# A mixed feed-forward phase in smaller parts, with its partial sums kept on the chip

## The reference

```python
h = relu(x @ gate_w1.T + gate_b1)
g = (h @ gate_w2.T + gate_b2).mean(axis=1)          # 8 numbers for each batch
mW1 = W1 + einsum('be,efh->bfh', g, TW1)            # mixed weights, one set for each batch
mb1 = b1 + g @ Tb1
mW2 = W2 + einsum('be,ehf->bhf', g, TW2)
mb2 = b2 + g @ Tb2
u = gelu(einsum('bsh,bfh->bsf', x, mW1) + mb1)
out = einsum('bsf,bhf->bsh', u, mW2) + mb2
result = x1 + layernorm(out)                        # x1: the residual; the network's x is layernorm(x1)
```

## Time and profile before

| | us |
|---|---|
| median of 3 runs | 3212.77 (3205.09 to 3214.96) |
| the profiled execution, its time | 3212.9 |
| its span, first to last instruction | 3210.9 |
| PE busy in the span | 2959.3 (92%) |
| DVE busy | 2125.1 (66%) |
| ACT busy | 1229.8 (38%) |
| POOL busy | 788.1 (25%) |

### The profile page before, as it was taken

The page is one execution under the profiler, slowest core; times in us unless marked ns, Lnnn a source line. Parts: engine busy times, 40 slices in busy tenths (PEclk is TensorE's granted clock), DMA queues, the critical chain, the costliest instruction groups (busy, mean ns, idle before and its releaser), DMA issues. The chain is left out here.

```text
span 3210.9 us, 54877 instructions
## 1 busy us (share of the span) xinstructions
PE 2959.3 (92%) x20408; PEld 2436.0 (76%) x20408; DVE 2125.1 (66%) x3970; ACT 1229.8 (38%) x2354; POOL 788.1 (25%) x629
## 2 busy tenths in 40 slices
PE   7999999699999999689979898689998999999997
PEld 6888888588888888567757777578877887778886
DVE  4333332388878888587678788586868858595633
ACT  2222222266666766555422222222323223322232
POOL 0000000288878888633200000100011000100011
PEclk9999999799999999889979999899999999999999
DMA  5545554678777777599989999787977959597631
GB/s 190 177 163 194 179 170 163 161 185 194 193 180 193 195 193 190 148 330 360 350 328 404 403 397 374 253 328 259 366 257 280 371 212 341 215 352 260 223 131 66
DMA packets 441120, 796.72 MB, mean 248 GB/s; under 512 B 29105, under 2 KB 161201, under 8 KB 440889
## 3 DMA queue, kind: packets, MB, share of 16 engines
q1 hardware_dynamic: 440896, 793.73, 73.8%
HBM read 600.16 MB, written 192.94 MB: 247 GB/s over the span
## 5 line engine op out<-in xcount | busy, mean ns | idle before, releaser
L1435 DVE SCALAR_TENSOR_TENSOR e_part<-ring,e_g_cols,e_part 128x512 f32<-128x512 f32 x896 | 634.4, 771 | 37.8 <-DMA ring<-mix_rows 37.5
L1379 ACT ACTIVATE e_u<-e_hid,e_mb 128x512 f32<-128x512 f32 x256 | 176.5, 689 | 966.9 <-PE e_hid L1327 966.7
L666 DVE TENSOR_REDUCE b_neg_max<-b_ps_score 128x1 f32<-128x384 f32 (+1 forms) x1024 | 492.3, 527 | 72.9 <-PE b_ps_score L531 61.2
L1341 PE MATMUL e_acc<-e_w_hi,e_u_hi 128*128 128x512 f32 x1024 | 417.2, 407 | 105.9 <-DVE e_u_lo L1445 105.9
L1286 POOL TENSOR_TENSOR e_rows<-e_rows,e_prev 128x512 f32<-128x512 f32 x64 | 96.9, 1543 | 1496.4 <-DVE e_rows L1473 994.7
L637 ACT ACTIVATE b_probs<-b_ps_keys 128x384 f32<-128x384 f32 (+1 forms) x1024 | 427.0, 478 | 84.5 <-PE b_ps_keys L546 57.0
L1325 PE MATMUL e_hid<-e_y_hi,e_w_hi 128*128 128x512 f32 x1024 | 401.9, 392 | 10.9 <-DMA e_y_lo<-yl_scratch 8.6
L1342 PE MATMUL e_acc<-e_w_lo,e_u_hi 128*128 128x512 f32 x1024 | 410.4, 401 | 0.0
L1343 PE MATMUL e_acc<-e_w_hi,e_u_lo 128*128 128x512 f32 x1024 | 410.1, 401 | 0.0
L1326 PE MATMUL e_hid<-e_y_lo,e_w_hi 128*128 128x512 f32 x1024 | 400.8, 391 | 0.0
L1327 PE MATMUL e_hid<-e_y_hi,e_w_lo 128*128 128x512 f32 x1024 | 400.1, 391 | 0.0
(11 more groups left out here) (118 smaller groups left out, 4797.0 us busy)
## 6 DMA issues: line engine op xcount, KB each, us to landing
ring<-mix_rows SPq DMA_DIRECT2D x576, 512.0 KB, 7.9
qk_scratch<-a_qk SPq DMA_DIRECT2D x128, 512.0 KB, 2.8
b_k_st<-qk_scratch SPq DMA_DIRECT2D x192, 256.0 KB, 4.3
b_q_st<-qk_scratch SPq DMA_DIRECT2D x192, 256.0 KB, 4.3
e_y_hi<-yh_scratch SPq DMA_DIRECT2D x40, 1024.0 KB, 9.5
e_y_lo<-yl_scratch SPq DMA_DIRECT2D x40, 1024.0 KB, 11.7
part_scratch<-e_rows SPq DMA_DIRECT2D x24, 1024.0 KB, 7.2
e_prev<-part_scratch SPq DMA_DIRECT2D x24, 1024.0 KB, 10.1
```

The lines of the kernel that those rows point to most:

```text
L666: dve.tensor_reduce(neg_max[:, g % 2, i, h:h + 1], ps_score[y % BANKS][:, 0:(hi - lo) * WIN], AX_X, ALU.max, negate=True).then_inc(reduced, 1)
L1341: pe.matmul(acc[t][:, :], u_hi[:, s % 2, cols], w_hi[:, slot, D:2 * D], start=begin, stop=False)
L1435: dve.scalar_tensor_tensor(out=part[:, n % 2, cols], in0=ring[:, i % RING, cols], scalar=g_cols[:, b, e:e + 1], in1=so_far, op0=ALU.mult, ...
```

## The change

1. The units become 3, 3, 3, 4 and 3 blocks in batch 0 and four times 4 in batches 1 to 3: 68 runs instead of 40. `RING` goes from 8 to 9 loads and `W_RING` from 12 to 9 blocks.
2. The earlier sums stay in SBUF (`sums`, all four chunks of a batch), and `part_scratch` is gone. At the end of a run ACT copies each `acc` to `sums` (`copy_out`), and before the next run it writes that run's earlier sum, or the bias on a batch's first unit, into `acc` (`preload`), on which the matmuls add up. DVE no longer touches `acc`.
3. A closing run's root is a power of -0.5 on POOL, with three other small instructions; the normalisation is on ACT, in place in `sums`; x1 has a buffer of its own.
4. PE is two blocks ahead: hidden(s+2), project(s). `u_hi` and `u_lo` have three buffers instead of two.
5. The first three blocks are mixed half by half. The bias of the second product is made for four rows, stored to HBM and loaded back to all partitions.
6. A run's y is loaded one step before the end of the run two earlier, behind that step's refills. Before, it was loaded at the first step of the run before it, ahead of that step's refills.

```diff
-RING = 8
-W_RING = 12
+RING = 9
+W_RING = 9
 def ffn_units():
-    return [(0, 0, 3), (0, 3, 4), (0, 7, 5), (0, 12, 4)] + [(b, 8 * half, 8) for b in range(1, BATCH) for half in range(2)]
+    return [(0, 0, 3), (0, 3, 3), (0, 6, 3), (0, 9, 4), (0, 13, 3)] + \
+        [(b, 4 * quarter, 4) for b in range(1, BATCH) for quarter in range(4)]
...
                 def load_y(r):
                     if r >= 2:
-                        sp.wait_ge(hid_done, first[r - 1])
+                        sp.wait_ge(hid_done, last[r - 2] + 1)
...
+                load_y(0)
+                sp.wait_ge(bias_done, BATCH + 1)
+                sp.dma_start(mb2_dram, mb2_rows).then_inc(mb2_stored, 16)
+                sp.wait_ge(mb2_stored, 16)
+                load_bias(0)
                 refill(0, EXPERTS)
-                load_y(0)
-                refill(EXPERTS, 2 * EXPERTS)
                 load_y(1)
-                refill(2 * EXPERTS, EXPERTS * START)
+                refill(EXPERTS, EXPERTS * START)
                 for s, (r, jj) in enumerate(steps):
-                    if jj == 0 and r >= 1:
-                        if closes(r - 1):
-                            load_x1(r - 1)
-                        else:
-                            store_part(r - 1)
-                    if jj == 0 and 2 <= r + 1 < RUNS:
-                        load_y(r + 1)
-                    if jj == 1 and not opens(r) and not closes(r - 1):
-                        load_prev(r)
                     refill(upto[s - 1] if s else EXPERTS * START, upto[s])
-                    if jj == 3 and r >= 1 and closes(r - 1):
-                        store_out(r - 1)
-                        if not opens(r):
-                            load_prev(r)
+                    for run in range(RUNS):
+                        if s == last[run] - 1 and run + 2 < RUNS:
+                            load_y(run + 2)
+                        if s == last[run] and closes(run):
+                            load_x1(run)
+                        if s == last[run] + 5 and closes(run):
+                            store_out(run)
...
             def _(pool):
+                        pool.tensor_scalar(var[:, :], moments[:, :, 1], EPS, None, ALU.add).then_inc(var_done, 1)
+                        pool.tensor_tensor(rstd[:, :], var[:, :], power[:, :], ALU.pow).then_inc(rstd_done, 1)
+                        pool.tensor_tensor(shift[:, 0, :], moments[:, :, 0], rstd[:, :], ALU.mult).then_inc(product_done, 1)
+                        pool.tensor_scalar(shift[:, 1, :], shift[:, 0, :], -1.0, None, ALU.mult).then_inc(shift_done, 1)
...
             def _(pe):
-                for r in range(RUNS):
-                    hidden(first[r])
-                    for s in range(first[r] + 1, last[r] + 1):
-                        hidden(s)
-                        project(s - 1)
-                    project(last[r])
+                for s in range(AHEAD):
+                    hidden(s)
+                for s in range(STEPS):
+                    if s + AHEAD < STEPS:
+                        hidden(s + AHEAD)
+                    project(s)
...
+                def copy_out(r, t):
+                    act.wait_ge(used, TILES * last[r] + t + 1)
+                    act.activation(sums[:, runs[r][1], t, :], acc[t][:, :], ACT.Copy).then_inc(copied, 1)
+
+                def preload(r, t):
+                    act.activation(acc[t][:, :], src, ACT.Copy).then_inc(preloaded, 1)
+
+                def normalise(r):
+                    act.wait_ge(shift_done, at + 1)
+                        act.activation(rows, rows, ACT.Identity, bias=shift[:, 1, t:t + 1], scale=rstd[:, t:t + 1]).then_inc(norm_done, 1)
...
             def _(dve):
+                for s in range(STEPS):
+                    if s + AHEAD < STEPS:
+                        low_hidden(s + AHEAD)
+                    for r in range(RUNS):
+                        if s == last[r] + 1 and closes(r):
+                            row_stats(r)
                     ops = list(range(upto[s - 1] if s else EXPERTS * START, upto[s]))
                     for m in ops[:1]:
-                        mix(m)
+                        mix_both(m)
                     for n in finished(s - 1):
                         low_weights(n)
```

More of the change, by code:

```diff
@@ L1047, in mix_plan @@
             last.append(len(blocks) - 1)
[L1048 to L1051, removed]
+            closing.append(j0 + nj == FF // P)
+    freed = {n: s for s, n in enumerate(blocks)}
     total = BATCH * FF // P
-    start = units[0][2]
     upto, done, spare = [], {}, 0.0
-    m = EXPERTS * start
+    m = EXPERTS * units[0][2]
     for s in range(len(blocks)):
[L1057 to L1063, removed]
+        cost = 0.8 + (3.4 if s - 1 in last and closing[last.index(s - 1)] else 0.0)
+        spare = min(spare + 5.44 - cost, 6.0)
         ops = 0
-        while spare > 1.35 and ops < 3 and m < EXPERTS * total:
+        while spare > 1.5 and ops < 3 and m < EXPERTS * total:
             n = m // EXPERTS
-            if m % EXPERTS == EXPERTS - 1 and n >= W_RING and freed[n - W_RING] > s - 1:
+            if m % EXPERTS == EXPERTS - 1 and n >= W_RING and freed[n - W_RING] > s:
                 break
@@ L1143, in phase_ffn @@
         u = sb("u", [P, 2, CH], F32)
[L1144 to L1147, removed]
+        u_hi = sb("u_hi", [P, 3, CH], F32R)
+        u_lo = sb("u_lo", [P, 3, CH], F32R)
+        sums = sb("sums", [P, PER, TILES, D], F32)
+        x1 = sb("x1", [P, TILES, D], F32)
+        bias = sb("bias", [P, D], F32)
         mb1 = sb("mb1", [P, BATCH, BLOCKS], F32)
-        mb2 = sb("mb2", [P, BATCH, D], F32)
         b1_sb = sb("b1", [P, BLOCKS], F32)
@@ L1235, in store_out @@
                         sp.wait_ge(added, TILES * closed_before(r) + t + 1)
-                        sp.dma_start(out[at:at + P, :], rows[:, t, :]).then_inc(rows_stored, 16)
+                        sp.dma_start(out[at:at + P, :], sums[:, runs[r][1], t, :]).then_inc(out_stored, 16)
                 def refill(m0, m1):
@@ L1273, in _ @@
+                for run in range(RUNS):
+                    if last[run] + 5 >= STEPS and closes(run):
+                        store_out(run)
+                sp.wait_ge(out_stored, 16 * TILES * PER * BATCH)
             @block.gpsimd
             def _(pool):
-                pool.memset(eps[:, :], EPS).then_inc(const_done, 1)
+                pool.memset(power[:, :], -0.5).then_inc(const_done, 1)
                 pool.memset(ident[:, :], 0.0).then_inc(const_done, 1)
@@ L1308, in biases @@
                     mm.then_inc(bias_psum, 1)
-                    for b in range(BATCH):
-                        mm = pe.matmul(acc[b][:, :], g_wide[:, b, :], tb2_sb, start=True, stop=True)
-                        mm.then_inc(bias_psum, 1)
+                    pe.matmul(hid[3][0:BATCH, :], g[:, :], tb2_sb, start=True, stop=True).then_inc(bias_psum, 1)
                 def hidden(s):
@@ L1454, in rows_out, with row_stats @@
+                def row_stats(r):
+                    at = closed_before(r)
+                    if at:
+                        dve.wait_ge(norm_done, TILES * at)
                     for t in range(TILES):
-                        more = mb2[:, batch_of(r), :] if opens(r) else prev[:, t, :]
-                        dve.tensor_tensor(rows[:, t, :], acc[t][:, :], more, ALU.add).then_inc(rows_done, 1)
-                def rows_stats(r):
-                    dve.wait_ge(rows_done, TILES * (r + 1))
+                        dve.wait_ge(copied, TILES * r + t + 1)
+                        dve.bn_stats(stats[:, t, :], sums[:, runs[r][1], t, :]).then_inc(stats_chain, 1)
@@ new lines, in _ @@
+                for n in range(START):
+                    for half in range(2):
+                        for e in range(EXPERTS):
+                            mix(n, e, half)
+                            if (n or half) and e == 1:
+                                low_half(*((n, 0) if half else (n - 1, 1)))
+                            if n == 0 and half == 0 and e == 3:
+                                biases()
+                low_half(START - 1, 1)
+                for s in range(AHEAD):
+                    low_hidden(s)
```

269 lines of the change are left out of this document (140 added, 129 removed).

## The result

The changed kernel takes 3229.65 us (median of 14 runs, 3220.62 to 3244.95), the kernel before 3208.48 (14 runs, 3201.76 to 3215.67) on the same chips: ratio 1.0065, 95% interval 1.0051 to 1.0079. It is slower by 0.65%, where 2.7% faster was forecast, and lies outside the range. Its profiled execution has a span of 3233.4 us at a granted clock of 0.954.

What follows compares the result with a forecast made beforehand. PE was taken as the bound, losing some 148 us to `u_lo` waits and low clock. Last matmul 3056.3 without waits, plus 2 cold clock, 47 y, 8 closing runs, 12 end: span 3125.3, time 3127 us, range 3078 to 3188.

Steps and rivals of the forecast that it cites:

- y: PE's new wait at run starts: y lands at 15.8 us, 15 runs of three wait 3.1 each, 47 us (14 to 90).
- DVE around closing runs: POOL's additions slow DVE's mixing at closing runs; mostly hidden by two blocks of lead, 8 us (0 to 25).
- y is in time: Rival, chance 0.20: with a short DMA queue y_lo lands sooner, runs of three wait 0.8 us, 12 us in all; 3092.
- stalls that go: PE's waits for `u_lo` and the low clock behind them count as gone, about 146 us.
- ACT at a boundary: Eight moves of 0.60 us between runs end at 3.6 us, before PE needs the fourth bank at 4.7; no cost.
- start: Before the first project: biases delay DVE and SP's refills; it begins at 1671.9 instead of 1662.1 (1662 to 1678).
- clock: PE's low clock behind waits, some 40 us, goes; 2 us for the cold start and 0.7 per y wait are added.
- second price: Skill's DMA page: 2.0 us plus bytes at 436 GB/s; y pair lands 6.8 us after issue, no run waits; 3080.
- runs of four don't notice it: Within the y term: y is there at 15.8 us, and PE in runs of four needs it at 18.9.
- The end: From the last matmul to the end of the span, 12 us (10 to 15).
- y is late everywhere, and DVE too: Rival, chance 0.15: y_lo takes 13.0 us to land; runs of three and some 36 of four wait; 3185, at worst 3220.

Runs made afterwards that it cites:

- e1: The changed kernel with only SP's order altered: y of run + 2 is asked for ahead of the same step's refills, one step sooner; 3090.69 us.
- e8: Against the changed kernel with y asked for one step sooner: ACT takes the square root again and POOL's power only inverts it; 3095.96 us.
- e5: Against the changed kernel with y asked for one step sooner: hidden runs one block ahead of project instead of two; 3104.39 us.

## Why the prediction was wrong

**Which step failed.** The term "*y*" of the sum (47 us), with "*DVE around closing runs*" (8 us). With y in time the rest of the sum gives what the rival "y is in time" had, 3092; e1 measures 3090.7. So stalls that go, ACT at a boundary, start and clock were right together, to within 2 us, and the whole miss of 103 us is y. A little of the 2 us is luck: e1's first project came 0.9 us sooner than forecast, 19.0 us were lost from there to the last matmul instead of 22, and the end took 13.3 us instead of 12.

**y in runs of three, 47 us, in fact 96** (443 - 347). The waits are 67.9 us in 15 places, 4.5 each where I had 2.4. The time of the issue was right where no run closes: 6.6 us after the gelu on average over these eleven (5.6 to 8.1), forecast 6.4. Three things were too small.

- The landing. I took 9.4 us (8.7 to 10.4), because the partial sum ahead of y was gone; it is 10.7. The runs of three all lie in batch 0, where the earlier trace rows have 13.0; less 2.6 that is 10.4, and the 11.3 that pulled it down is of the later batches. So these eleven wait 6.6 + 10.7 - 13.4 = 3.9 us. By the issues and landings in the trace 2.1 to 2.6 MB are outstanding when y_lo is asked for, y_hi's 1 MB among them, and refills follow it. The "load of 1 MB with nothing before it" of 5.7 us, on which the rival "y is in time" rests, is the store of a partial sum in the earlier trace rows; y_hi took 8.3 us here.
- The four loads asked for while closing runs go on. They are asked for 8.1, 6.7, 9.2 and 14.1 us after the gelu, and PE waits 6.4 us for them on average, 11.5 for the last.
- The clock. I added 0.7 us for a clock that sometimes falls. Each of these 15 waits has a stretch at 0.50 beside it, of 3.4 to 13.7 us; none of e1's nine waits of up to 2.2 us has one. PE's busy time in batch 0 is 31.5 us longer than in e1 for as many matmuls, 2.1 us a wait.

The rule of the Trainium skill that I had as a second price (DMA: Bandwidth & Descriptors, Anatomy of one DMA: 2.0 us and the bytes), is the furthest off here: applied to the pair alone, as I did, it has y_lo landed after an estimated 6.8 us.

**Around closing runs, 8 us, in fact some 46** more than in e1 (19, 16 and 11 us in the last three batches). I priced the slower mixing as DVE's own lag and hid it behind two blocks. The lag doesn't reach PE through `u_lo`, as I had it, but through SP: y stands behind the refills, these behind the mixing. What I called "runs of four don't notice it" leaves 18.9 - 15.8 = 3.1 us of room, and four slow instructions (5.85 instead of 2.74) with a slow `w_lo` (2.31 instead of 1.22) are 4.2 us: 12.3 us to the issue in place of 8.1, the most that I allowed. The room, 3.1 us, and the slow mixing, 4.77 us for four, were both in the prediction, and I didn't put them together. Here the Trainium skill's page (SBUF — State Buffer, Who interferes with whom) pointed the right way: by it VectorE's instruction and GpSimd's block each other, and the rows have 5.85 us for the four beside additions that take 7.41, where the earlier trace rows have 4.92.

**The start** came as worked out (first project 1671.0 in e1, 1674.7 in the changed kernel, forecast 1671.9). **The end** takes 13.5 us from the last matmul (3219.84 to 3233.4), not 12: the load of `x1` for the last run is asked for at 3219.11, behind POOL's previous additions, and POOL waits 2.49 us for it. **The boundary**: moves take 0.60 us, PE never waits for them. **The root**: worth 5 us (e8).

**What I gave to the wrong cause.** "With two hidden blocks ahead, a late `u_lo` has 5.4 us more before PE notices" was to clear 146 us. e5 shows that with the rest of the change a lead of one clears nearly all of it, and that the second block is worth 14. The lead is also what brings the loss: it needs y a step earlier, and SP's order wasn't moved with it. In the prediction that stood as "PE needs it one run later less 2.9", so it was counted. What wasn't asked is why y was issued so late, when the buffer was free a step before.

Of the rivals, the nearest was "y is late everywhere, and DVE too" (chance 0.15; 3185, at the worst 3220), but by its time and not by its mechanism: it assumed 13.0 us of landing, which was 10.7, and a wait in every run of four with mixing in front. Those wait only around closing runs, where y is asked for late.

## What to carry to other kernels

When a change lets one engine run further ahead, list every load that this engine needs and see that each is asked for as much sooner: here one place in the order of SP's queue was worth 139 us. Without it the change loses 21 us, with it it gains 118. A load that stands behind waits in an in-order queue inherits the delay of all that these wait for, so its slack is to be checked where those are slowest, not in the steady state. And price a short wait of TensorE with the slower matmuls behind it, which here added half of the wait's own length.

## What was not expected of the hardware

During a wait of 3.04 us the granted clock fell to 0.50, where it stayed for 6.8 us. The changed kernel has 94.7 us more of waits for y than e1_y_early, and they cost it 142 us. The load of y_lo took as long at 299 GB/s (10.7 us, 1690 to 2100 of the changed kernel, 2.1 to 2.6 MB outstanding at most of its issues) as at 374 GB/s (10.9 us, e1_y_early, 1690 to 2010, 2.6 to 4.7 MB). What sets it stays open; it wasn't tried alone.
